# Attention 1 of a two-layer kernel: q and k turned once per feature block in the projection, stacks of the heads filled by SBUF transfers, another order of the pieces, values in halves

## The chip, the cores and the metric

One core of a Trainium2 chip (trn2) runs the whole program. The metric is the device time of one execution in microseconds. The kernel before takes 2137.48 us, the median of 3 runs (2134.89 to 2144.37). Five engines work side by side and meet at semaphores: TensorE (PE; its weight loads are PEld), VectorE (DVE), ScalarE (ACT), GpSimd (POOL) and SyncE (SP), whose queue issues the transfers, one after the other.

## The reference

Two transformer layers on a hidden state of 1 x 1024 x 512 float32: a decayed linear attention, a gated feed-forward with LoRA, a causal softmax attention with ALiBi and a normalisation of q and k, and a feed-forward with GELU. The change is in the third of these, which is

```python
qkv = clip(hidden @ w_qkv.T, -8, 8)             # 512 features each, 32 heads of 16
q = layer_norm(q, q_ln_w, q_ln_b)               # over all 512 features, then split into heads
k = layer_norm(k, k_ln_w, k_ln_b)
scores = q @ k.T / sqrt(16) + alibi_bias        # per head, 1024 x 1024, causal
out = softmax(scores) @ v                       # then @ w_out.T
```

## The kernel before

`stage_attention1` (L822) has three blocks with their own semaphores and a barrier between them: `attention1_qkv` (L836), `attention1_heads` (L1074) and `attention1_out` (L1443).

**Projection, `attention1_qkv`.** 24 tiles m (8 token tiles each for q, k, v) of 128 tokens by 512 features. PE makes a tile with 12 matmuls into PSUM bank m % 8. DVE clips it into `cl` (L944) and takes the moments (L947, L949); POOL makes 1/std and shift in three tiny operations (`moments`, L890 to L894); ACT normalises (L923); POOL multiplies by the weight (`scale`, L899), DVE adds the bias (`shift`, L935) and so writes `q1` and `k1`, tokens on partitions. v is clipped straight into `v1` (L951). POOL also splits each of the three weight matrices into a high and a low part (`split`, L876): that of v comes at m == 3 of the loop over moments.

**Heads, `attention1_heads`.** The 32 heads go in 16 pairs p and 8 quads g (pairs 2g and 2g + 1). For a pair there is a stack `KTs[p % 5]` and a stack `QT[p % 5]`: 128 rows by 1024 tokens, 64 rows for each head: 16 rows of slopes, positions and the row maximum (row `MAXROW`), and three times 16 rows of high and low parts of k or q. A stack is made in three steps: POOL's `gather` (L1126) puts the columns of the pair, split, beside the constants in `ks`, `qs`, tokens on partitions, two pairs per quad; PE's `turn` (L1310) transposes them in 16 transposes (L1318) into a score slot `S[at % 2]`; ACT's `turned` (L1176) copies each to its stack (L1182). A score slot is two PSUM banks, and there are two of them, shared with the scores.

For each pair the row maxima come first. PE makes 24 `piece`s (L1345, matmul at L1354) of 128 queries by up to 512 keys into one of three banks `M[at % 3]`; DVE takes each one's maximum (L1239 with the causal mask on the diagonal, L1243 without). After the last piece DVE combines them (L1247), PE transposes the result (`max_row`, L1363), DVE copies it to `crow` (L1256), and SP writes it by two transfers (L1121) into row MAXROW of `QT`. Only then may the scores of that pair start: `score` (L1322) waits for `max_in` at n == 0.

A quad has 12 steps n (key tile by query range, `STEPS`) times 2 pairs = 24 units u. Unit u: PE makes the scores of two heads (L1334), ACT takes exp into `pr[n % 4]` (L1193), POOL zeroes the triangle of a diagonal step (`select`, L1158), and PE multiplies by `v1` (`values`, L1385: 8 passes for 4 heads side by side in the array, into bank `O`). Between the units PE issues the pieces of the pairs 2g + 2 and 2g + 3, from the generator `maxima(g)`, as many per unit as `paced(g)` says. ACT copies `O` out twice a quad (L1201), PE transposes it (L1371), DVE divides (L1265, L1268). Before the first quad come the turns of pairs 0, 1, 2 and the pieces of pairs 0 and 1: the prologue. Every engine takes its instructions strictly in the order written.

Of the kernel before, what the change touches and what calls it, by code (L numbers as in the profile page):

```python
# [821 lines left out]
def stage_attention1(nc, top, a):  # L822

    ctx = ExitStack()
    with ctx:
        def sb(name, shape, dt=F32):
            return ctx.enter_context(nc.sbuf_tensor(f"a1_{name}", shape, dt))
        q1, k1 = sb("q1", [P, NT, D]), sb("k1", [P, NT, D])
        v1 = sb("v1", [P, NT, H1, DH1 + 1])
        attention1_qkv(nc, top, q1, k1, v1, a["a1_wqkv"], a["a1_ln"])  # L830
        attn = sb("attn", [P, NT, D])
        attention1_heads(nc, top, q1, k1, v1, attn, a)
        attention1_out(nc, top, attn, a["a1_wout"])


def attention1_qkv(nc, top, q1, k1, v1, w_dram, ln_dram):  # L836
# [3 lines left out]
    with ctx:  # L840
# [7 lines left out]
        wb = sb("wb", [P, 4, D])  # L848
        R = 4
        FIRST = 3  # L850
        cl = sb("cl", [P, R, D])
        st, mv = sb("st", [P, R, 6]), sb("mv", [P, R, 2])
# [5 lines left out]
        def whole(m):  # L858

            return (q1, k1)[m // NT][:, m % NT, :]  # L860
# [4 lines left out]
        def _(sp):  # L865
            for c in range(3):
# [3 lines left out]
                if c == 0:  # L870
                    for i in range(4):
                        sp.dma_start(wb[:, i, :], ln_dram[i:i + 1, :].to_broadcast([P, D])).then_inc(s("wb_in"), 16)

        @block.gpsimd
        def _(pool):
# [21 lines left out]
            def scale(m):  # L897
                pool.wait_ge(s("normed"), m + 1)
                nc.gpsimd.tensor_tensor(cl[:, m % R, :], cl[:, m % R, :], wb[:, 2 * (m // NT), :], ALU.mult  # L899
                                        ).then_inc(s("scaled"), 1)  # L900
# [6 lines left out]
            pool.wait_ge(s("wb_in"), 64)  # L907
            for m in range(QK + 1):
                if m < QK:
                    moments(m)  # L910
                if m >= 1:
                    scale(m - 1)
                if m == 3:
                    pool.wait_ge(s("proj_done"), NT)
                    split(2)

        @block.scalar
        def _(act):
            ln_scalar(nc, act, s, b)
            for m in range(QK):  # L920
                r = m % R
                act.wait_ge(s("sh"), m + 1)
                nc.scalar.activation(cl[:, r, :], cl[:, r, :], ACT.Identity, bias=sh[:, r:r + 1],  # L923
                                     scale=rs[:, r:r + 1]).then_inc(s("normed"), 1)

        @block.vector
        def _(dve):
# [3 lines left out]
            dve.wait_ge(s("wb_in"), 64)  # L931

            def shift(m):
                dve.wait_ge(s("scaled"), m + 1)
# [858 lines left out]
```

## Time and profile before

| | us |
|---|---|
| median of 3 runs (lowest, highest) | 2137.48 (2134.89, 2144.37) |
| the profiled execution, its time | 2137.82 |
| its span, first to last instruction | 2136.1 |
| projection of attention 1, from its weights' DMA to its last DVE instruction | 1425.1 to 1517.8 |
| prologue of the heads, from SP's first DMA to the first score | 1519.0 to 1560.3 |
| quad 0 to quad 7, from the first score to the last output | 1560.3 to 1893.8 |
| PE, DVE, ACT, POOL busy over the span | 93%, 41%, 21%, 39% |

The page has a line for each engine with its busy time, the span in 40 slices with the clock that TensorE was granted (full is 2.4 GHz; the records know this level and 1.2 GHz), the waits, and the groups of instructions by line. A line of a timeline gives the start, the busy time and, in brackets, how long the engine was idle before it and who released it. "issue to landing" is the time from the start of a DMA instruction on SP to the last byte's semaphore.

### The profile page before, as it was taken

What the parts mean: (1) busy time and instruction counts of PE and PEld (TensorE: products, weight loads), DVE (VectorE), ACT (ScalarE), POOL (GpSimd) and SP (SyncE); (2) the same over time, 40 slices, a digit from 0 to 9 for tenths busy, and PEclk for the clock granted to TensorE, in tenths of its full rate; (3) what the DMA queues carried; (4) which work ended last, traced back from release to release, by engine and by line L of the source; (5) the groups of instructions that cost most, each with busy time, mean ns of one, the idle gap of its engine ahead of it and who ended that gap; (6) DMA issues with size and microseconds to landing.
All of it is one profiled execution on the core that took longest, in us unless ns stands there. A gap on an engine that the chain in (4) does not pass through costs nothing. (4 is left out here: it accounts for less than half of the span.)

```text
span 2136.1 us, 27055 instructions
## 1 busy us (share of the span) xinstructions
PE 1987.8 (93%) x10154; PEld 1538.6 (72%) x10154; DVE 875.7 (41%) x1593; ACT 453.2 (21%) x550; POOL 831.7 (39%) x1164
## 2 busy tenths in 40 slices
PE   6999999999999999999996799979699889887998
PEld 5888888888888888888885577757444444355877
DVE  4242442323424334243245433335565666524232
ACT  3111111111111111111110200012135555532111
POOL 4331321322313122223000688868513232127765
PEclk9999999999999999999999899989769888897999
DMA  4110110101001101011001233321100000002333
GB/s 149 38 45 28 55 55 27 54 27 54 30 24 54 54 27 54 27 54 34 7 12 40 73 106 96 110 71 40 18 1 1 1 2 1 2 20 77 91 93 99
DMA packets 47564, 98.90 MB, mean 46 GB/s; under 512 B 12976, under 2 KB 17712, under 8 KB 43024
## 3 DMA queue, kind: packets, MB, share of 16 engines
q1 hardware_dynamic: 47504, 98.12, 14.4%
q8 instruction: 36, 0.59, 0.1%
q14 instruction: 24, 0.20, 0.0%
HBM read 95.87 MB, written 2.10 MB: 46 GB/s over the span
## 5 line engine op out<-in xcount | busy, mean ns | idle before, releaser
L60 POOL TENSOR_TENSOR tick<-neg_half 128x1 f32<-128x1 f32 x188 | 53.4, 284 | 669.5 <-PE a_ps L148 615.5
L146 PE MATMUL a_ps<-a_xh_h,a_w_h 128*128 128x512 f32 x768 | 307.4, 400 | 4.6 <-POOL a_w_l L270 3.2
L148 PE MATMUL a_ps<-a_xh_h,a_w_l 128*128 128x512 f32 x768 | 301.6, 393 | 0.0
L147 PE MATMUL a_ps<-a_xh_l,a_w_h 128*128 128x512 f32 x768 | 300.7, 392 | 0.0
L390 DVE TENSOR_TENSOR x<-x,a_ps 128x1024 f32<-128x1024 f32 x64 | 78.2, 1221 | 259.9 <-PE a_ps L148 259.9
L1193 ACT ACTIVATE a1h_pr<-a1h_ps 128x1024 f32<-128x1024 f32 (+1 forms) x192 | 150.0, 811 | 154.7 <-PE a1h_ps L1334 128.5
L146 PEld LDWEIGHTS a_ps<-a_xh_h,a_w_h 128*128 128x128 f32 x768 | 145.0, 189 | 32.8 <-issue 3.5
L148 PEld LDWEIGHTS a_ps<-a_xh_h,a_w_l 128*128 128x128 f32 x768 | 144.5, 188 | 30.4
L147 PEld LDWEIGHTS a_ps<-a_xh_l,a_w_h 128*128 128x128 f32 x768 | 144.9, 189 | 28.0
L1158 POOL TENSOR_SCALAR_AFFINE_SELECT a1h_pr<-a1h_pr 128x256 f32<-128x256 f32 x128 | 51.6, 407 | 261.4 <-ACT a1h_pr L1193 260.6
L1354 PE MATMUL a1h_ps<-a1h_KT,a1h_QT 64*128 64x512 f32 (+2 forms) x384 | 127.8, 472 | 17.6 <-DVE a1h_mx L1243 5.9
L1239 DVE CUSTOM_DVE_ANT_0 a1h_masked<-a1h_ps,a1h_mask 128x128 f32<-128x128 f32 (+3 forms) x256 | 112.9, 485 | 71.0 <-PE a1h_ps L1354 70.5
L372 DVE SCALAR_TENSOR_TENSOR a_gt<-a_th,a_ps 128x1024 f32<-128x1024 f32 x32 | 39.1, 1221 | 234.3 <-ACT a_sq L307 234.3
L251 POOL TENSOR_TENSOR a_w_l<-a_raw,a_w_h 128x2048 fp32r<-128x2048 f32 x29 | 133.7, 4609 | 2.4
L146 PE MATMUL f_ps<-f_xh_h,f_w_h 128*128 128x512 f32 x304 | 121.6, 400 | 7.6 <-DVE f_low_st L728 3.1
L147 PE MATMUL f_ps<-f_xh_l,f_w_h 128*128 128x512 f32 x304 | 121.1, 398 | 0.0
L148 PE MATMUL f_ps<-f_xh_h,f_w_l 128*128 128x512 f32 x304 | 120.8, 397 | 0.0
L316 ACT ACTIVATE a_qT<-a_ps 128x1024 f32<-128x1024 f32 x32 | 32.8, 1024 | 397.4 <-PE a_ps L148 397.4
L1354 PEld LDWEIGHTS a1h_ps<-a1h_KT,a1h_QT 64*128 64x128 f32 x384 | 66.2, 222 | 61.0 <-DVE a1h_mx L1239 24.7
L1334 PEld LDWEIGHTS a1h_ps<-a1h_QT,a1h_KT 64*128 64x128 f32 x384 | 44.5, 217 | 91.0 <-issue 38.4
L146 PE MATMUL a_ps<-a_o_h,a_g_h 128*128 128x512 f32 x256 | 102.9, 402 | 6.2 <-DVE a_g_l L381 5.6
L1243 DVE TENSOR_REDUCE a1h_mx<-a1h_ps 128x1 f32<-128x512 f32 x128 | 84.4, 687 | 55.8 <-PE a1h_ps L1354 55.8
(191 smaller groups left out, 4147.8 us busy)
## 6 DMA issues: line engine op xcount, KB each, us to landing
a_raw<-in_a_wqkgv SPq DMA_DIRECT2D x30, 1024.0 KB, 5.1
f_raw<-in_f_w SPq DMA_DIRECT2D x66, 320.0 KB, 3.1
f_raw<-in_f_w SPq DMA_DIRECT2D x64, 256.0 KB, 2.6
a_raw<-in_a_wout SPq DMA_DIRECT2D x32, 256.0 KB, 5.1
a_cst<-in_a_cst SPq DMA_DIRECT2D x32, 129.0 KB, 2.1
a1q_raw<-in_a_wqkv SPq DMA_DIRECT2D x3, 1024.0 KB, 4.9
x<-in_x_in SPq DMA_DIRECT2D x8, 256.0 KB, 3.8
a_v_nat<-in_a_wqkgv SPq DMA_DIRECT2D x2, 1024.0 KB, 10.6
```

Source lines behind the costliest of these rows:

```text
L60: nc.gpsimd.tensor_tensor(top["tick"][:, :], top["neg_half"][:, 0:1], top["neg_half"][:, 1:2], ALU.mult)
L146: nc.tensor.matmul(out, w_hi, x_hi, start=start, stop=False)
L147: nc.tensor.matmul(out, w_hi, x_lo, start=False, stop=False)
L148: return nc.tensor.matmul(out, w_lo, x_hi, start=False, stop=stop)
L251: nc.gpsimd.tensor_tensor(w_l[:, j, :], raw[:, 0:W4], w_h[:, j, :], ALU.subtract).then_inc(s("w_ready"), 1)
L390: nc.vector.tensor_tensor(a, a, UNIT[(i + 1) % 2], ALU.add).then_inc(s("out_added"), 1)
L1158: nc.gpsimd.affine_select(tri, tri, [[0, 2], [1, P]], ALU.is_ge, 0.0, base=0, channel_multiplier=-1).then_inc(s("selected"), 1)
L1193: nc.scalar.activation(pr[n % SLOTS][:, 2 * i:2 * i + 2, 0:width], S[at % 2][:, :, skip:skip + width], ACT.Exp, scale=0.25).then_inc(s("sc ...
L1239: nc.vector.tensor_tensor_reduce(out=masked[:, at % 3, 0:width], in0=M[at % 3][:, 0:width], in1=mask[:, BANK - width:], scale=-1.0, scalar ...
L1243: nc.vector.tensor_reduce(to, M[at % 3][:, 0:width], AX.X, ALU.max, negate=True).then_inc(s("max_taken"), 1)
L1334: last = nc.tensor.matmul(out[:, h, 0:w], KTs[p % SETS][rows, kt * P:(kt + 1) * P], QT[p % SETS][rows, q0 + width - w:q0 + width], start=True,
L1354: nc.tensor.matmul(out[:, 0:w], QT[p % SETS][rows, t * P:(t + 1) * P], KTs[p % SETS][rows, c * BANK:c * BANK + w], start=True, stop=True). ...
```

## The change

**Projection.** `scale` and `shift` go. ACT's normalised tiles stay in `cl` (8 slots instead of 4). For four token tiles and one block of 128 features PE makes a `turn` of four transposes into one of two banks (PROJ + u % 2); 16 such units, placed after tiles m = 7, 8, 10, 11, 14, 15, 18, 19, two after each. ACT applies weight and bias, now one number per partition, and writes the high part (`high`); DVE makes the full value (`whole`); POOL subtracts (`low`). Result: `q_h`, `q_l`, `k_h`, `k_l`, features on partitions. The projection uses 6 banks instead of 8. v's `split` comes at m == 8.

**Heads.** `gather`, the 16 transposes per pair and the two ACT copies go. SP's `stack(p)` fills the stacks by transfers from SBUF to SBUF of 16 rows by 4 KB: 12 per pair, and 4 of 2 or 3 rows for the slopes; for the first five pairs also 4 of 16 rows with the constants, with two waits for them. `max_row(p)` of SP keeps its two transfers; both stand on the same queue. Pieces alternate wide and narrow; the prologue holds the first 8 pieces of pair 2 (AHEAD), and each quad works 8 pieces ahead. `values` of wide steps is made in two halves at units u - 3. `masked` is bf16.

```diff
 def attention1_qkv(...)
-        R = 4
+        R = 8
         FIRST = 3
+        PROJ = 6
+            def low(u):
+                pool.wait_ge(s("full"), u + 1)
+                nc.gpsimd.tensor_tensor(target(u, "_l"), full[:, u % 2, :], target(u, "_h"), ALU.subtract
+                                        ).then_inc(s("turned_lo"), 1)
-            for m in range(QK + 1):
-                if m < QK:
-                    moments(m)
-                if m >= 1:
-                    scale(m - 1)
-                if m == 3:
+            for m in range(QK):
+                moments(m)
+                for u in units(m):
+                    low(u)
+                if m == 8:
                     pool.wait_ge(s("proj_done"), NT)
                     split(2)
+            def whole(u):
...
+                if u >= 2:
+                    dve.wait_ge(s("turned_lo"), u - 1)
+                nc.vector.tensor_scalar(full[:, u % 2, :], ps[:, PROJ + u % 2, :], wb[:, 2 * c, feature:feature + 1],
+            def turn(u):
+                _, first, feature = TURNS[u]
+                pe.wait_ge(s("normed"), first + 4)
+                if u >= 2:
+                    pe.wait_ge(s("full"), u - 1)
...
+                if m >= PROJ:
+                    pe.wait_ge(s("clipped"), m - PROJ + 1)
                 for k in range(KT):
                     part(m, k)
+                for u in units(m):
+                    turn(u)
```

```diff
 def attention1_heads(...)
+            def stack(p):
+
+                if p >= PAIRS:
+                    return
+                if p >= SETS:
+                    g, i = divmod(p - SETS, 2)
+                    sp.wait_ge(s("score_made"), score_at(g, NS - 1, i) + 1)
+                    sp.wait_ge(s("max_made"), MAX_AT[(p - SETS, NP - 1)] + 1)
+                landed = s(f"stack_in{p % SETS}")
+                for h in range(2):
...
+                    for n, (k, q) in enumerate((("k_h", "q_h"), ("k_l", "q_h"), ("k_h", "q_l"))):
+                        sp.dma_start(kT[at[n]:at[n + 1], :], turned[k].bitcast(F32)[rows, block, :]).then_inc(landed, 16)
+                        sp.dma_start(qT[at[n]:at[n + 1], :], turned[q].bitcast(F32)[rows, block, :]).then_inc(landed, 16)
+                    if p == 0 and h == 0:
+                        sp.wait_ge(s("slopes_round"), 2)
+                    e, r = 2 * p + h, ROWS * h
+                    if p < SETS:
+                        sp.dma_start(kT[r:r + AUG, :], qslope.bitcast(F32)[KBASE:KBASE + AUG, :]).then_inc(s("base_in"), 16)
+                        sp.dma_start(qT[r:r + AUG, :], qslope.bitcast(F32)[QBASE:QBASE + AUG, :]).then_inc(s("base_in"), 16)
+                        sp.wait_ge(s("base_in"), 32 * e + 32)
+                    sp.dma_start(kT[r + 3:r + 5, :], kslope.bitcast(F32)[2 * e:2 * e + 2, :]).then_inc(landed, 16)
+                    sp.dma_start(qT[r:r + 3, :], qslope.bitcast(F32)[3 * e:3 * e + 3, :]).then_inc(landed, 16)
...
+            sp.dma_start(raw[0][:, :], a["a1_qslope"]).then_inc(s("slope_in"), 16)
+            sp.dma_start(raw[1][0:2 * H1, :], a["a1_kslope"]).then_inc(s("slope_in"), 16)
+            stack(0)
+            sp.dma_start(mask[:, :], a["a1_mask"]).then_inc(s("mask_in"), 16)
+            sp.dma_start(later[:, :], a["a1_later"]).then_inc(s("later_in"), 16)
+            for p in range(1, SETS):
+                stack(p)
+            max_row(0)
+            max_row(1)
+            for g in range(QUADS - 1):
+                max_row(2 * g + 2)
+                stack(2 * g + 5)
+                max_row(2 * g + 3)
+                stack(2 * g + 6)
...
 PE, within a quad: for u, upto in enumerate(paced(g))
                     score(g, n, i)
-                    if u == 0:
-                        turn(2 * g + 3)
-                    for _ in range(upto - made):
+                    for _ in range((upto - made + 1) // 2):
+                        next(strand)
+                    before = (u - 3) // 2
+                    if before >= 0:
+                        values(g, before, (u - 3) % 2)
+                    elif g:
+                        values(g - 1, NS + before, (u - 3) % 2)
+                    for _ in range((upto - made) // 2):
                         next(strand)
                     made = upto
-                    if i == 0 and n >= 2:
-                        values(g, n - 2)
...
-                    if u == 15:
-                        turn(2 * g + 4)
...
             def maxima(g):
+                yield from pieces(p, AHEAD, 16)
                 if g:
                     yield output(g - 1, 1)
+                yield from pieces(p, 16, NP)
                 yield from pieces(q, 0, 2)
                 if p < PAIRS:
                     yield max_row(p)
+                yield from pieces(q, 2, 8)
                 yield output(g, 0)
+                yield from pieces(q, 8, NP)
+                yield from pieces(q + 1, 0, 2)
+                if q < PAIRS:
+                    yield max_row(q)
+                yield from pieces(q + 1, 2, AHEAD)
```

## Rows read from the trace of the kernel before

**Rows 1.** The page: span, busy times, and granted clock in tenths by slice of the span.

```profile
span 2136.1 us, 27055 instructions
...
PE 1987.8 (93%) x10154; PEld 1538.6 (72%) x10154; DVE 875.7 (41%) x1593; ACT 453.2 (21%) x550; POOL 831.7 (39%) x1164
...
PEclk9999999999999999999999899989769888897999
```

**Rows 2.** Busy time by stretch: stretch, length, engines with counts, granted clock, DMA.

```profile
1518.90:1560.30 41.40, 29.61 (x97) 18.85 (x98) 22.66 (x81) 7.96 (x9) 13.68 (x40) 0.62 0.18 23
1560.30:1617.10 56.80, 54.67 (x283) 26.15 (x282) 30.79 (x108) 26.34 (x32) 13.70 (x37) 0.73 0.00 1
1617.10:1658.60 41.50, 37.20 (x234) 17.72 (x234) 26.29 (x89) 23.33 (x30) 13.30 (x36) 0.88 0.01 2
...
1826.30:1866.10 39.80, 33.63 (x194) 13.76 (x194) 23.22 (x74) 19.41 (x26) 6.46 (x16) 0.79 0.00 1
1866.10:1893.80 27.70, 22.49 (x162) 7.79 (x162) 1.74 (x6) 18.61 (x26) 6.01 (x15) 0.88 0.00 1
```

**Rows 3.** Who waited for whom, 1617 to 1866: total us, times, longest.

```profile
ACT a1h_pr L1193 <- PE a1h_ps L1334: 110.6, 78, 4.1
DVE a1h_mx L1243 <- PE a1h_ps L1354: 44.2, 48, 2.7
DVE a1h_masked L1239 <- PE a1h_ps L1354: 38.1, 28, 3.9
```

**Rows 4.** Groups by line, 1617 to 1866: count, busy, mean ns, idle before.

```profile
L1318 PE MATMUL a1h_ps<-ident,a1h_ks 128*128 128x128 f32 x80 | 11.0, 281 | 1.1 <-ACT a1h_pr L1193 1.1
L1318 PE MATMUL a1h_ps<-ident,a1h_qs 128*128 128x128 f32 x80 | 10.8, 278 | 0.0
L1182 ACT CAST a1h_KT<-a1h_ps 128x1024 fp32r<-128x1024 f32 x10 | 10.1, 1012 | 2.8 <-PE a1h_ps L1318 2.8
```

**Rows 5.** Timeline of PE and DVE: the projection, its end, the first turn.

```profile
1453.66 0.60 PE L139 MATMUL a1q_ps<-ident,a1q_xn 128*128 128x128 f32 x4
1454.02 0.48 PE L146 MATMUL a1q_ps<-a1q_w_h,a1q_xh_h 128*128 128x512 f32 x1
...
1509.37 0.39 PE L148 MATMUL a1q_ps<-a1q_w_h,a1q_xh_l 128*128 128x512 f32 x1
...
1514.08 3.67 DVE L951 TENSOR_SCALAR a_v<-a1q_ps 128x512 f32<-128x512 f32 x6
...
1527.23 1.94 PE L1318 MATMUL a1h_ps<-ident,a1h_ks 128*128 128x128 f32 x8 [17.48 <-POOL a1h_qs L1152]
...
1532.61 0.50 PE L1354 MATMUL a1h_ps<-a1h_KT,a1h_QT 64*128 64x256 f32 x3
```

**Rows 6.** Groups by line and shape in the projection, 1425 to 1518.

```profile
L899 POOL TENSOR_TENSOR a1q_cl<-a1q_cl,a1q_wb 128x512 f32<-128x512 f32 x16 | 20.5, 1286 | 0.0
...
L944 DVE TENSOR_SCALAR a1q_cl<-a1q_ps 128x512 f32<-128x512 f32 x16 | 10.9, 679 | 0.0
...
L54 POOL TENSOR_SCALAR a1q_w_h<-a1q_raw 128x512 fp32r<-128x512 f32 x12 | 7.5, 621 | 2.1 <-DMA a1q_raw<-in_a_wqkv 2.1
```

**Rows 7.** Timeline of SP: start, time of the group of issues, line, count.

```profile
1.72 3.28 SPq L201 DMA_DIRECT2D x<-in_x_in  x7
...
1863.66 1.31 SPq L1121 DMA_DIRECT2D a1h_QT<-a1h_crow  x2
```

**Rows 8.** DMA issues of the whole span: count, KB each, us to landing.

```profile
a1h_mask<-in_a_mask SPq DMA_DIRECT2D x1, 256.0 KB, 3.9
...
a1h_later<-in_a_later SPq DMA_DIRECT2D x1, 64.0 KB, 2.5
```

**Rows 9.** Timeline of PE: a score behind its row of maxima, and values of two widths.

```profile
1712.66 0.63 PE L1385 MATMUL a1h_ps<-a1h_pr,a_v 128*17 128x256 f32 x8
...
1734.37 1.05 PE L1385 MATMUL a1h_ps<-a1h_pr,a_v 128*17 128x512 f32 x8
...
1866.13 0.68 PE L1334 MATMUL a1h_ps<-a1h_QT,a1h_KT 64*128 64x512 f32 x4 [2.27 <-DMA a1h_QT<-a1h_crow]
```

More of the change, by code:

```diff
@@ L856, in attention1_qkv, with units, target @@
         QK = 2 * NT
-        def whole(m):
-            return (q1, k1)[m // NT][:, m % NT, :]
+        def units(m):
+            return [u for u, (at, _, _) in enumerate(TURNS) if at == m]
+        def target(u, part):
+            _, first, feature = TURNS[u]
+            c, t = first // NT, first % NT
+            return turned["qk"[c] + part][:, feature, t * P:t * P + BANK]
         by_head = lambda ap: ap.rearrange("p (h d) -> p h d", h=H1)
@@ L1003, with count @@
 NP = len(PIECES)
+AHEAD = 8
 def counted():
[L1008 to L1016 removed]
+    at = {}
+    def count(*item):
+        at[item] = len(at)
     def pieces(p, k0, k1):
         for k in range(k0, k1 if p < PAIRS else k0):
[L1020 to L1026 removed]
+            count(p, k)
@@ L1027, in counted @@
     pieces(0, 0, NP)
     pieces(1, 0, 2)
-    other("row", 0)
+    count("row", 0)
     pieces(1, 2, NP)
+    pieces(2, 0, 2)
+    count("row", 1)
+    pieces(2, 2, AHEAD)
     for g in range(QUADS):
-        for n in range(NS):
-            score(g, n, 0)
-            if n == 0:
-                turned(2 * g + 3)
-            score(g, n, 1)
-            if n == 7:
-                turned(2 * g + 4)
         p, q = 2 * g + 2, 2 * g + 3
-        pieces(p, 0, 2)
-        other("row", 2 * g + 1)
-        pieces(p, 2, 18)
+        pieces(p, AHEAD, 16)
@@ L1043, in counted @@
         if g:
-            other("out", g - 1, 1)
-        pieces(p, 18, NP)
+            count("out", g - 1, 1)
+        pieces(p, 16, NP)
         pieces(q, 0, 2)
         if p < PAIRS:
-            other("row", p)
-        pieces(q, 2, 10)
-        other("out", g, 0)
-        pieces(q, 10, NP)
-    other("out", QUADS - 1, 1)
-    return score_at, max_at
-SCORE_AT, MAX_AT = counted()
-def paced(g):
-    first = MAX_AT[("row", 2 * g + 1)] - (2 if g < QUADS - 1 else 0)
-    last = MAX_AT[("row", 2 * g + 3)] - 2 if g < QUADS - 2 else MAX_AT[("row", 2 * g + 3)] if g < QUADS - 1 else len(MAX_AT) - 1
-    worth = [PIECES[i[1]][3] + 80 if isinstance(i[0], int) else 300 for i in list(MAX_AT)[first:last]]
-    marks = [sum(worth[:i]) / sum(worth) for i in range(len(worth))]
-    length = 2 * sum(2 * n + 100 for _, _, n in STEPS)
-    upto, now = [], 1500
+            count("row", p)
@@ new lines, in counted @@
+        pieces(q, 2, 8)
+        count("out", g, 0)
+        pieces(q, 8, NP)
+        pieces(q + 1, 0, 2)
+        if q < PAIRS:
+            count("row", q)
+        pieces(q + 1, 2, AHEAD)
+    count("out", QUADS - 1, 1)
+    return at
+MAX_AT = counted()
+def paced(g):
+    if g == QUADS - 1:
+        return [0] * 3 + [1] * 9 + [2] * 12
+    items = list(MAX_AT)
+    first = MAX_AT[(2 * g + 2, AHEAD)]
+    last = MAX_AT[(2 * g + 4, AHEAD)] if g < QUADS - 2 else MAX_AT[("row", 2 * g + 3)] + 1
+    worth = [PIECES[i[1]][3] + 70 if isinstance(i[0], int) else 350 for i in items[first:last]]
+    length = sum(2 * n + 100 for _, _, n in STEPS) * 2
+    upto, now = [], 0
@@ L1069, in paced, with attention1_heads @@
             now += 2 * n + 100
-            upto.append(sum(m * length < now for m in marks))
-    return upto[:-1] + [len(marks)]
-def attention1_heads(nc, top, q1, k1, v1, attn, a):
+            upto.append(sum(sum(worth[:i]) * length < now * sum(worth) for i in range(len(worth))))
+    return upto
+def attention1_heads(nc, top, turned, v1, attn, a):
     ctx = ExitStack()
@@ L1205, in _ @@
             nc.scalar.copy(laterb[:, :], later[:, :]).then_inc(s("later_ready"), 1)
-            for p in range(3):
-                turned(p)
             for g in range(QUADS):
@@ L1417, in _ @@
             max_row(0)
-            turn(2)
             for k in range(2, NP):
                 piece(1, k)
+            piece(2, 0)
+            piece(2, 1)
+            max_row(1)
+            for k in range(2, AHEAD):
+                piece(2, k)
             for g in range(QUADS):
```

294 lines of the change are left out of this document (124 added, 170 removed).

## Prediction

> **What bounds the kernel now.** I read the page first [rows 1]. PE is busy 93% of the span, the others 41% and less, so PE's order of work sets the end. The clock line gives 9 nearly everywhere and falls to 7 and 6 in slices 29 and 30 and in some slices behind them: that is the attention the change is about. The table by stretch splits it [rows 2]: a prologue of 41.4 us, quad 0 of 56.8 us, quads like the one shown of 41.5 us (1617.1 to 1826.3 is five of them, 209.2 us), quad 6 of 39.8 and quad 7 of 27.7 us. In a quad of 41.5 us PE is busy 37.2, DVE 26.3, ACT 23.3 us. PE's busy time there counts the latency of matmuls that come singly, so it is no proof of a full array; the waits say what happens [rows 3]: ACT waits for scores 110.6 us and DVE for pieces 44.2 + 38.1 = 82.3 us of 249. Both starve behind PE's one ordered stream, in which turns, scores, values and pieces take turns. PE's order bounds the quads; in the prologue DVE's maxima do (22.7 us busy of 41.4, nearly all after the first turn), and before them a hole of 17.5 us in PE between the last projection matmul and the first turn [rows 5].
>
> **Projection.** PE's last matmul ends at 1509.8, DVE's last clip at 1517.75, 8 us behind [rows 5]. The change adds 16 units of four transposes to PE. Four transposes keep it 0.36 us from the next matmul (1453.66 to 1454.02) and 0.60 us if it must let them finish [rows 5]: 5.8 to 9.6 us; I take 5.8, since matmuls follow most units. DVE loses 16 adds and gains 16 reads of a bank, each like the clip of 0.68 us [rows 6], and this comes out even. POOL loses 16 multiplications of 1.29 us and gains 16 subtractions of the same shape and price [rows 6]. But they come in twos, and the split of v, four times 0.62 + 1.29 = 7.6 us [rows 6], now stands at m = 8 with the moments of tiles 9 to 11 queued behind it on POOL. DVE's `whole` waits for `low` and holds the clips behind it; PE's turn at m = 14 waits for normalised tile 11. I put 3 us of PE's waits there, between 0 and 6. PE then ends at 1509.8 + 5.8 + 3 = 1518.6, and DVE's last clip (0.68) right behind it, at 1519: against 1517.75 it is +1 us, between -2 and +4. The smaller weight and bias transfers lie beside the layer norm: nothing either way.
>
> **Prologue: what SP must issue before the first score.** This is the heart. Before, the first score starts at 1560.3. After, SP's queue reads: two loads, stack(0), two loads, stacks 1 to 4, and only then max_row(0) and max_row(1). The first score waits for the row of pair 0. Durations: an issue takes 3.28/7 = 0.47 us for 128 rows of 2 KB, and 1.31/2 = 0.66 us for the one kind that goes from SBUF to SBUF [rows 7]. The trace has no transfer of 16 rows by 4 KB. Its bounds are 0.34 (an estimate: under the nearer row by as much as 128 rows cost more than 16, if a quarter of the 0.47 goes with the rows) and 0.66; I take 0.46, because it is as plain in its pattern as those of 0.47, and 0.66 for the two slope transfers of a head. A wait for landing: 64 KB from DRAM land 2.5 us after their issue began [rows 8]; the row of maxima lets its score start at 1866.13, 2.47 us after its pair of transfers began at 1863.66 [rows 7, 9]. I take 2.0 us for 64 KB inside SBUF, so 1.5 us beyond the issue itself. A head in the first five pairs: 8 x 0.46 + 1.5 + 2 x 0.66 = 6.5 us; a stack 13.0 us. Stack(0) starts with six issues and waits until POOL has rounded the slopes: loads issued at 1519.0 and 1519.5 of 512 and 256 KB land in about 4 us (256 KB: 3.9 [rows 8]), two operations of twice 0.62 us [rows 6], so 1526.5; then 2 x 0.46 + 1.5 + 2 x 0.66 = 3.7 us to finish that head, 6.5 us for the other: 1536.7; two loads, 0.9: 1537.6; four stacks, 52: 1589.6; the row of pair 0, 2.5: **the first score at about 1592, 32 us later than now.** DVE doesn't reach this: 56 pieces instead of 48 at (1560.3 - 1532.6)/48 = 0.58 us [rows 2, 5], from 1540 when the mask is in, would be over at 1573. With 0.34 us an issue, 16 x 0.12 less five times, it is 1582; with 0.66 us, 16 x 0.2 more five times, 1608. The gather, six turns and six copies of the prologue cost nothing any more, but the hole they made is replaced by this longer one.
>
> **A quad, without waits for SP.** PE loses the turns: (11.0 + 10.8)/5 = 4.4 us of 37.2 busy. ACT loses four copies of 1.01 us, 4.05 us [rows 4], and with them two waits of the score slots. Values in halves add work: two halves of 256 take 2 x 0.63 against 1.05 us for 512 [rows 9], 0.2 us at most for each of eight wide steps, 0 to 1.7 us; the lower end is likely, since the halves stand between pieces. In return PE comes back to the scores and pieces sooner. Floors: DVE 26.3 us; ACT 23.3 - 4.05 = 19.3 us. Ceiling: 41.5 - 4.4 = 37.1 us, where no wait goes. I take 33 us, PE's remaining busy time 32.8 us with idle and saved latency even; between 28.5 (DVE nearly full) and 37.1. `masked` in bf16 and POOL without gather: nothing, because DVE's operation reads PSUM at the same width and POOL's gather stood beside the quads, not in their way.
>
> **The new wait in each quad.** On SP, stack(2g + 5) waits for the last score of pair 2g, the unit before the last of quad g, then issues 16 transfers: 12 x 0.46 + 4 x 0.66 = 8.2 us. The row of pair 2g + 3 is queued behind it, and its 2.5 us come on top: 10.7 us after that score. Yet score(g + 1, 0, 1), the second unit of the next quad, waits for this row. Until there PE has one score, the next quad's first score, three halves of values and some six pieces, which DVE takes at 0.58 us: 3.5 us. PE stalls some 7 us, and DVE, ACT and the rest of the values are queued behind it. A stall of this length has a price in clock: after the hole of 17.5 us the stretch is granted 0.62, and quad 0 0.73, against 0.88 later [rows 2, 5]. I add 2 us (0 to 4). This happens behind quads 0 to 5; for g = 6 there is no stack to issue. With issues of 0.34 to 0.66 us, the stall is 5 to 10.
>
> **The sum.** Prologue +32. Quad 0: 33 + 9 + 3 for the low clock at its start = 45 against 56.8: -11.8. Quads 1 to 5: 42 against 41.84: +0.8. Quad 6: 34 against 39.8: -5.8. Quad 7, without pieces and mostly ACT's: 26 against 27.7: -1.7. Projection +1. Together +14.5 us. The execution profiled took 2137.82 us (the median is 2137.48; I leave out the 0.3): **2152 us**.
>
> **The rivals.**
> *A, DVE becomes the bound (the other side: faster).* If finer interleaving fills DVE, a quad goes at 28.5 us. For it: DVE idles 82 us in six quads only because PE serves it in lumps [rows 3]. Against it: PE in order, clock at 0.88. Seven quads save 4.5 us each: 2152 - 31.5 = 2120.5. The whole is faster than now if a quad without waits goes under 31.0 us, and counts as faster by over 0.5% under 29.4.
> *B, a transfer of 16 rows is dearer than a plain one.* For it: the only SBUF to SBUF rows cost 0.66 us [rows 7]. Then a stack of the prologue takes 3.2 us more, five times, and each stall 2.4 us more, six times: +30, 2182 us. The Trainium skill has a mechanism that would do the same: by its page SBUF — State Buffer, Door 1: The DMA port swizzle, a transfer's rate goes with how many of 16 ports its partitions reach, and 16 neighbouring partitions reach 4, some 109 GB/s. An estimate by that page is 0.60 us for 64 KB, longer than the issue that I took, and the sum would be near 2173; no row here shows a transfer of so few long rows.
> *C, quads don't shrink beyond PE's own saving.* Each takes 37.1 us, as ACT's waits for scores stay [rows 3]: +4.1 us seven times, 2181 us.
>
> **How the numbers follow.** Forecast 0.45, with 2136 to 2168 of its own; A 0.25; B 0.15; C 0.15. About 0.5% (10.7 us) is what a measurement of this kernel can tell from no change. Faster by more: A, less a little: 0.24. Within: the lower part of the forecast's range, up to 2148, and A's edge: 0.21. Slower by more: the rest of the forecast, B, C: 0.55. The range has to reach both sides: from 2112, A with most of its width, to 2190, B and C with theirs; less than 2 in 10 stays outside.
>
> **What would show it.** SP's timeline: 16 issues between the last score of pair 2g and the transfers of `crow`; right if a stack takes 7 to 9 us, wrong under 5.5. PE's waits: score L1334 of the second unit, released by the DMA of `crow`, some 7 us six times, and none behind quad 6; if these are missing, the main term is wrong. The first score at 1582 to 1608. Between the stalls, a quad of 33 us by the table of stretches; at 29 A has it, at 37 C. Timeline of the projection: PE's waits at m = 14 for `a1q_cl`. Clock by stretch: under 0.8 behind each stall. The prediction fails if transfers land so that the row is never last, or if DVE, not SP, still releases the first score.

## The result and the profile after the change

The changed kernel takes **2193.66 us** (median of 4 runs, 2192.41 to 2196.30), the kernel before 2137.81 us in the same comparison (4 runs): the ratio is 1.0259 [1.0233, 1.0284]. The forecast was 2152 us in a range of 2112 to 2190: the sign is right, the time forecast is 42 us short, and the time lies just past the range.

The page of the changed kernel, with two groups of its section on the costliest:

```profile
span 2190.9 us, 27811 instructions
...
PE 1952.5 (89%) x10474; PEld 1519.5 (69%) x10474; DVE 878.3 (40%) x1593; ACT 438.4 (20%) x534; POOL 773.7 (35%) x1006
...
PEclk9999999999999999999997999989558878887999
...
L1346 PE MATMUL a1h_ps<-a1h_QT,a1h_KT 64*128 64x512 f32 (+2 forms) x384 | 114.8, 457 | 91.7 <-DMA a1h_QT<-a1h_crow 91.3
...
L1366 PE MATMUL a1h_ps<-a1h_KT,a1h_QT 64*128 64x512 f32 (+2 forms) x384 | 143.4, 482 | 42.8 <-DMA a1h_QT<-a1h_qslope 32.1
```

PE is busy 35 us less than in [rows 1], and the span is 54.8 us longer: PE has less to do and waits. Scores (L1346) wait 91.3 us for `crow`, pieces (L1366) 32.1 us for a stack. The clock row shows two slices at 5, where before the lowest was 6.

The table by stretch, with the columns of [rows 2]: prologue, quad 0, two of the quads 1 to 5, quad 6, and quad 7 (its last 3 us lie behind the quad). As in [rows 2], every boundary behind the prologue is the score of a quad's second unit, so each stall lies at the end of the stretch before it:

```profile
1527.10:1618.60 91.50, 26.09 (x58) 14.36 (x58) 28.55 (x99) 1.88 (x3) 2.05 (x2) 0.52 0.41 72
1618.60:1673.70 55.10, 44.66 (x291) 19.56 (x291) 28.52 (x90) 20.96 (x26) 6.95 (x17) 0.72 0.10 17
1673.70:1717.00 43.30, 32.26 (x266) 14.75 (x266) 26.19 (x88) 20.20 (x26) 6.53 (x16) 0.82 0.24 40
...
1846.70:1890.00 43.30, 32.28 (x265) 14.62 (x266) 25.98 (x86) 20.21 (x26) 6.53 (x16) 0.82 0.24 40
1890.00:1921.80 31.80, 29.74 (x258) 12.96 (x258) 21.85 (x74) 19.58 (x26) 6.12 (x15) 0.88 0.01 2
1921.80:1950.00 28.20, 24.88 (x229) 9.66 (x230) 2.05 (x6) 19.21 (x27) 6.53 (x16) 0.86 0.01 1
```

Set beside [rows 2], the whole difference can be laid out. Each entry is the stretch after less the stretch before. Quad 7 ends at ScalarE's last copy of an output, which starts at 1892.06 us before and at 1946.78 us after. The changed kernel's projection began 2.1 us sooner in this execution (its first transposition at 1426.41 us, before at 1428.54, and between 1427.3 and 1430.3 in the runs below), so the stage itself grew by 10.3 us.

| stretch | forecast | measured | how |
|---|---|---|---|
| projection | +1 | +8.2 | 1527.1 - 1518.9 |
| prologue | +32 | +50.1 | 91.5 - 41.4 |
| quad 0 | -11.8 | -1.7 | 55.1 - 56.8 |
| quads 1 to 5 | +0.8 | +7.1 | 216.3 - 209.2 |
| quad 6 | -5.8 | -8.0 | 31.8 - 39.8 |
| quad 7 | -1.7 | -1.0 | 25.0 - 26.0 |
| sum | +14.5 | +54.7 | the spans differ by 54.8 |

The timeline of PE shows the two long waits of the prologue, then the second and the sixth of the waits for a row that end a quad; there are six of 10.1 to 10.5 us, and behind quad 6 one of 0.2:

```profile
1550.36 0.98 PE L1366 MATMUL a1h_ps<-a1h_KT,a1h_QT 64*128 64x512 f32 x3 [25.04 <-DMA a1h_QT<-a1h_qslope]
...
1618.67 0.80 PE L1346 MATMUL a1h_ps<-a1h_QT,a1h_KT 64*128 64x512 f32 x2 [29.69 <-DMA a1h_QT<-a1h_crow]
...
1717.05 0.80 PE L1346 MATMUL a1h_ps<-a1h_QT,a1h_KT 64*128 64x512 f32 x2 [10.19 <-DMA a1h_QT<-a1h_crow]
...
1890.00 0.80 PE L1346 MATMUL a1h_ps<-a1h_QT,a1h_KT 64*128 64x512 f32 x2 [10.20 <-DMA a1h_QT<-a1h_crow]
```

The timeline of SP shows what stands ahead of them: in the prologue (first load, first constant rows after POOL has rounded the slopes, the mask behind stack 0, the rows of pairs 0 and 1), and in a quad (first and last issue of a stack, then the row):

```profile
1527.12 0.33 SPq L1177 DMA_DIRECT2D a_attn<-in_a_qslope  x1
...
1536.24 0.51 SPq L1164 DMA_DIRECT2D a1h_KT<-a1h_qslope  x1
...
1548.87 0.41 SPq L1180 DMA_DIRECT2D a1h_mask<-in_a_mask  x1
...
1616.18 2.68 SPq L1174 DMA_DIRECT2D a1h_QT<-a1h_crow  x4
...
1704.24 0.55 SPq L1158 DMA_DIRECT2D a1h_KT<-a_k_h  x1
...
1713.81 0.69 SPq L1168 DMA_DIRECT2D a1h_QT<-a1h_qslope  x1
1714.54 1.34 SPq L1174 DMA_DIRECT2D a1h_QT<-a1h_crow  x2
```

A transfer of 16 rows is issued every 0.60 to 0.63 us. A stack of a quad takes 1714.54 - 1704.24 = 10.3 us, and the score starts 2.5 us behind the issue of its row. Of the 91.5 us of the prologue, 21.8 pass up to the mask, 66.4 with the four other stacks (from 1549.8), and 2.5 with the row.

### The profile page after: what moved, and what is told of

Same layout as the page of the kernel before. It is cut to its first block and busy times, and to the rows that moved or that the text cites. A ratio compares the mean times of both kernels' runs of the same rounds, so it can differ in the third digit from the quotient of the medians.

```text
span 2190.9 us, 27811 instructions
## 1 busy us (share of the span) xinstructions
PE 1952.5 (89%) x10474; PEld 1519.5 (69%) x10474; DVE 878.3 (40%) x1593; ACT 438.4 (20%) x534; POOL 773.7 (35%) x1006
## 5 line engine op out<-in xcount | busy, mean ns | idle before, releaser
L1346 PE MATMUL a1h_ps<-a1h_QT,a1h_KT 64*128 64x512 f32 (+2 forms) x384 | 114.8, 457 | 91.7 <-DMA a1h_QT<-a1h_crow 91.3
L1366 PE MATMUL a1h_ps<-a1h_KT,a1h_QT 64*128 64x512 f32 (+2 forms) x384 | 143.4, 482 | 42.8 <-DMA a1h_QT<-a1h_qslope 32.1
L148 PEld LDWEIGHTS a_ps<-a_xh_h,a_w_l 128*128 128x128 f32 x768 | 144.4, 188 | 30.3
L1261 DVE CUSTOM_DVE_ANT_0 a1h_masked<-a1h_ps,a1h_mask 128x384 bf16<-128x384 f32 (+3 forms) x256 | 115.3, 486 | 99.2 <-PE a1h_ps L1366 98.1
L1366 PEld LDWEIGHTS a1h_ps<-a1h_KT,a1h_QT 64*128 64x128 f32 x384 | 72.7, 220 | 118.3 <-issue 49.9
L1346 PEld LDWEIGHTS a1h_ps<-a1h_QT,a1h_KT 64*128 64x128 f32 x384 | 55.3, 212 | 114.9 <-DMA a1h_QT<-a1h_crow 93.4
```

Of the source, the lines that this page charges most:

```text
L148: return nc.tensor.matmul(out, w_lo, x_hi, start=False, stop=stop)
L1261: nc.vector.tensor_tensor_reduce(out=masked[:, at % 3, 0:width], in0=M[at % 3][:, 0:width], in1=mask[:, BANK - width:], scale=-1.0, scalar ...
L1346: last = nc.tensor.matmul(out[:, h, 0:w], KTs[p % SETS][rows, kt * P:(kt + 1) * P], QT[p % SETS][rows, q0 + width - w:q0 + width], start=True,
L1366: nc.tensor.matmul(out[:, 0:w], QT[p % SETS][rows, t * P:(t + 1) * P], KTs[p % SETS][rows, c * BANK:c * BANK + w], start=True, stop=True). ...
```

## The experiments

**What an issue costs.** The kernel before, with unused transfers in series on SP in one quad; between series SP waits until all have landed.

```diff
+                for i in range(8):
+                    sp.dma_start(probe[16 * i:16 * i + 16, 1, :], probe[0:16, 0, :]).then_inc(s("probe_in"), 16)
+                sp.wait_ge(s("probe_in"), 16 * 8)
+                for i in range(8):
+                    sp.dma_start(probe[16 * i:16 * i + 16, 1, :], d[0][0:16, 0:1024]).then_inc(s("probe_in"), 16)
...
```

> The kernel before with transfers added that nothing uses, on SP in quad 1, where its queue is idle: 8 of 16 rows by 4 KB from SBUF to SBUF, 8 of 16 rows by 4 KB from DRAM, 4 of 128 rows by 4 KB from SBUF, 4 of 128 rows by 4 KB from DRAM, 4 of 64 rows from SBUF, 8 of 16 rows by 256 bytes from SBUF, 4 of 2 rows by 4 KB from SBUF; SP waits for each series to land. Nothing of the kernel's own work waits for them, as long as the whole series takes under 35 us. Theory S (the source decides the issue): both series from DRAM take 0.45 us an issue, all from SBUF 0.63. Theory N (the number of rows decides): 128 rows take 0.45, from either side, and 16 rows 0.63, from either side. Theory D (the data hold the issue up): 256-byte rows are issued in under 0.5 us, 4 KB rows in 0.63.

The timeline of SP; a row is a series, its second number the time from its first issue to the end of its last. The shapes are 16 rows of 4 KB out of SBUF, the same out of DRAM, 128 rows of 4 KB out of SBUF and out of DRAM, 64 rows of 4 KB, 16 rows of 256 B and 2 rows of 4 KB, the last three out of SBUF:

```profile
1613.38 5.94 SPq L1122 DMA_DIRECT2D a1h_probe<-a1h_probe  x8
1621.05 3.59 SPq L1125 DMA_DIRECT2D a1h_probe<-in_a_wqkv  x8
1626.42 3.27 SPq L1128 DMA_DIRECT2D a1h_probe<-a1h_probe  x4
1633.26 1.90 SPq L1131 DMA_DIRECT2D a1h_probe<-in_a_wqkv  x4
1641.83 3.17 SPq L1134 DMA_DIRECT2D a1h_probe<-a1h_probe  x4
1648.53 4.98 SPq L1137 DMA_DIRECT2D a1h_probe<-a1h_probe  x8
1654.61 2.47 SPq L1140 DMA_DIRECT2D a1h_probe<-a1h_probe  x4
```

Divided by the count: 0.74, 0.45, 0.82, 0.48, 0.79, 0.62 and 0.62 us. Out of DRAM the pitch is 0.45 to 0.48, whether 64 or 512 KB. Out of SBUF it is 0.62 even for 4 KB, and more where much is moved. So it is the source that sets the least price of an issue, not the number or length of the rows: theory S. It is one execution, and why its series of 64 KB goes at 0.74 us where the stacks' transfers of the same size go at 0.60 to 0.63 was not tried. The forecast's 0.46 was the price of the wrong source; the floor of rival B (0.66, the one kind from SBUF) was the right neighbour.

**The row ahead of the stack.** One pair of lines in SP's loop changes places; nothing else.

```diff
-                stack(2 * g + 5)
                 max_row(2 * g + 3)
+                stack(2 * g + 5)
                 stack(2 * g + 6)
```

> The kernel after, with one line moved on SP: in the loop over quads max_row(2g + 3) stands ahead of stack(2g + 5) instead of behind it. Theory Q (the queue: the second score of a quad waits because 16 transfers of 0.63 us stand ahead of its row of maxima): PE's six waits of 10.2 us at the second unit go down to under 1 us each, a quad goes from 43.3 to about 33 us, and the time from 2193.7 to about 2132 us, 61 us less. Rival R (the quads are long for another reason, and the wait only collects what PE would lose to DVE, ACT or late stacks): the wait moves to another line, the quads stay over 40 us and the time over 2175 us. The prologue stays as it is: first score near 1619 us.

2123.03 us, ratio to before 0.9926 [0.9898, 0.9954]: 70.6 us under the changed kernel. The six waits are gone; what is left of PE's waits for `crow` is the one at the first score. The waits, and two quads in the table by stretch:

```profile
PE a1h_ps L1346 <- DMA a1h_QT<-a1h_crow: 30.5, 2, 29.6
...
1686.90:1717.20 30.30, 28.96 (x260) 13.23 (x258) 25.57 (x88) 19.87 (x26) 6.50 (x16) 1.00 0.33 57
1717.20:1748.00 30.80, 29.48 (x269) 13.41 (x266) 26.11 (x88) 20.28 (x26) 6.50 (x16) 1.00 0.33 56
```

The waits removed were 91.3 - 30.5 = 60.8 us. The other 10 us go with the clock: a quad of 43.3 us less its wait of 10.2 is 33.1 us at a granted clock of 0.82, and here it is 30.3 to 30.8 us at 1.00; five such quads are 12 to 14 us. The chain from SP's queue over the row to the score is shown, and its price with it.

**The rows of the prologue earlier.** The rows of pairs 0 and 1 go behind stack 2 instead of behind stack 4.

```diff
-            for p in range(1, SETS):
-                stack(p)
+            stack(1)
+            stack(2)
             max_row(0)
             max_row(1)
+            stack(3)
+            stack(4)
```

> The kernel after, with the order of SP in the prologue changed: stack(1), stack(2), max_row(0), max_row(1), stack(3), stack(4), instead of the four stacks first. Theory Q: the first score is then released after stack 2 has landed (near 1584), two pieces, row 1 and its landing: at about 1590 instead of 1618.7, and the time falls by about 28 us, to 2165 us. Rival R (stacks 3 and 4 are needed early as well, or DVE's 56 pieces are what takes this long): the first score stays within 5 us of 1618, or the gain is lost again in quad 0; time over 2185 us. The six waits of 10 us between the quads stay in both.

2166.61 us, ratio 1.0127 [1.0098, 1.0155]: 27 us less than the changed kernel. The prologue, from SP's first load to the first score, takes 60.9 us (1530.77 to 1591.63) instead of 91.6 (1527.12 to 1618.67), 30.7 us less. In the prologue SP's queue is what the kernel waits for, and 27 of these 30.7 us come back in the time.

**Both orders.** 

> Both changes of SP's order, in one kernel. Theory Q: the two gains add, 61 + 28 us: about 2105 us, under the kernel before (2137.8) by 1.5%. Rival R: they don't add, because stacks 3 and 4 now land in quad 0 and hold its pieces: 2120 us or more.

2090.53 us, ratio 0.9768 [0.9740, 0.9796]: with two changes of order the changed kernel beats the kernel before by 2.3%. It is also 15 us below its own forecast of 2105, as the first order alone was 9 us below its 2132: both forecasts had counted the waits and left out what the quads behind them gain in clock. Its quad 0 and two quads behind it:

```profile
1591.60:1634.90 43.30, 42.99 (x271) 18.90 (x271) 27.57 (x89) 19.54 (x25) 6.11 (x15) 0.71 0.31 53
1634.90:1666.00 31.10, 29.76 (x268) 13.38 (x268) 25.81 (x86) 20.29 (x27) 6.42 (x16) 1.00 0.32 54
1666.00:1696.90 30.90, 29.54 (x271) 13.43 (x272) 26.09 (x88) 20.20 (x27) 6.52 (x17) 1.00 0.33 56
```

Quad 0 has no wait for a row here and is still 12.4 us longer than a quad behind it: PE is busy 43.0 against 29.5 us with as many matmuls (271), at 0.71. That goes with starting the quad on the lower of the two levels (1.2 GHz), on which PE had been through the prologue (busy 25.5 of 60.9 us, granted clock 0.50).

**Values whole, pieces by tile.** Two edits of the change taken back, each alone, on top of both orders.

```diff
-                whole = kt == 0 or width == P
+                whole = True
```

> The two edits of SP's order, and the products with the values of every step done whole, as before the change, instead of in halves between the scores. It prices the halves. A quad of the run with the order alone takes 30.7 us with TensorE busy 29.5, so whoever thinks the quad TensorE-bound expects no more than a microsecond in all: 2090 us (2088 to 2094). Rival (the halves give VectorE's maxima time between the scores and so made a part of the fall from 41.6 to 30.7 us): 1 us more for each of eight quads, 2099 us (2095 to 2105).

> The two edits of SP's order, and the pieces of maxima in the order of before, tile by tile. It prices the reordering. Theory (a quad without the wait is TensorE-bound at 29.5 of 30.7 us, and three banks of maxima smooth out single wide pieces): within 4 us, 2092 us (2088 to 2096). Rival (wide pieces in a row let VectorE, 0.4 to 0.7 us each, hold TensorE up at the banks): 2 us more in each of seven quads, 2105 us (2098 to 2112), with TensorE's waits for max_taken over 10 us in all.

For the second, `PIECES` is the list of before. Both are set against the kernel with both orders (2090.53 us, 0.9768 [0.9740, 0.9796]), of which they differ by that one edit. Values whole: 2110.39 us, ratio 0.9860 [0.9825, 0.9895], 20 us more. The rival had the direction, but less than half the size. Pieces by tile: 2099.19 us, ratio 0.9800 [0.9766, 0.9834]: 7 to 9 us more, but the intervals overlap, so that no price of the reordering is shown; the time lies between the two expectations. Values whole, by stretch:

```profile
1635.10:1667.80 32.70, 29.47 (x215) 13.05 (x215) 26.65 (x89) 20.31 (x27) 7.02 (x18) 1.00 0.32 53
...
1700.70:1734.70 34.00, 31.36 (x204) 13.45 (x202) 26.27 (x89) 19.92 (x26) 6.41 (x16) 0.90 0.30 50
```

Pieces by tile:

```profile
1667.20:1698.40 31.20, 29.35 (x268) 13.07 (x266) 26.34 (x88) 20.32 (x26) 6.41 (x17) 1.00 0.32 55
...
1764.00:1801.30 37.30, 35.95 (x268) 15.57 (x267) 26.26 (x88) 20.18 (x27) 6.37 (x16) 0.77 0.26 45
```

At full clock the halves are worth some 1.7 us a quad (32.7 against 30.9 to 31.1) and the order of the pieces 0.3 us (31.2 against 30.9). The rest of what was lost goes with the clock: with values whole PE was idle 3.2 us of the first quad shown instead of 1.3, and of the four behind it one was granted 0.95 and three 0.90, the one shown 1.3 us longer; with pieces by tile one late quad was granted 0.77 and took 37.3 us. The kernel with both orders has one such quad too, the fifth (0.95). That the additional idle time is what drew the clock down was not tested by itself.

**The split of v, tile by tile, in the projection.**

```diff
-                if m == 8:
+                if 8 <= m < 12:
                     pool.wait_ge(s("proj_done"), NT)
-                    split(2)
+                    split(2, (m - 8,))
```

In the changed kernel the chain is read from the timelines of four engines, from its end back to its start:

```profile
1486.47 0.87 PE L1002 MATMUL a1q_ps<-ident,a1q_cl 128*128 128x128 f32 x3 [6.52 <-DVE a1q_full L963]
...
1485.51 1.53 DVE L963 TENSOR_SCALAR a1q_full<-a1q_ps,a1q_wb 128x512 f32<-128x512 f32 x2 [7.51 <-ACT a_q_h L939]
...
1484.00 0.81 ACT L949 ACTIVATE a1q_cl<-a1q_cl,a1q_sh,a1q_rs 128x512 f32<-128x512 f32 x1 [10.79 <-POOL a1q_sh L905]
1484.72 1.43 ACT L939 ACTIVATE a_q_h<-a1q_ps,a1q_wb 128x512 fp32r<-128x512 f32 x2
...
1474.85 0.63 POOL L54 TENSOR_SCALAR a1q_w_h<-a1q_raw 128x512 fp32r<-128x512 f32 x1
...
1481.42 1.26 POOL L894 TENSOR_TENSOR a1q_w_l<-a1q_raw,a1q_w_h 128x512 fp32r<-128x512 f32 x1
1482.77 0.19 POOL L901 TENSOR_SCALAR a1q_ve<-a1q_mv 128x1 f32<-128x1 f32 x1
```

PE's turn (L1002, at m = 11) waits for `full` on DVE, that for `high` on ACT (L939), which is queued behind a normalisation (L949), which waits for POOL's moments (L901), which stand behind 7.8 us of splitting. The edit is made on top of both orders.

> Two edits of SP's order as in the run of 2090.5 us, and in the projection the split of v's weights on GpSimd taken apart: one tile of it (hi and lo) behind the moments of each of m = 8, 9, 10, 11, where all four stood behind those of m = 8. Theory P (the projection's growth of 7 us over the forecast is GpSimd's split of v standing ahead of the moments of m = 9, behind which ScalarE's turned copies queue and with them TensorE's turns): TensorE's wait of 8.0 us for a1q_full at the turn of m = 11 shrinks below 3 us, the heads' part starts about 5 us sooner, 2085 us (2082 to 2088). Rival (the wait is the length of the chain ScalarE high, VectorE full, GpSimd low per turn, whatever the split does): the same time is waited in smaller pieces, 2090 us (2088 to 2093).

PE's wait there falls from 8.0 us (in the kernel with both orders) to 2.2, its waits for `full` in all from 10.3 to 6.0. The first piece starts at 1548.92 instead of 1553.88, 4.96 us sooner; 0.7 us of this is a projection that began sooner, so that 4.3 us are left. The median does not show it: 2091.42 us, ratio 0.9778 [0.9739, 0.9818]. The spans of the profiled executions fell by 4.0 us (2093.2 to 2089.2). So the step is shown in the trace; its worth in time is not, and three pairs of profiled executions, below, are what there is.

**One landing wait for the constant rows of a stack.** On top of both orders; the first five stacks send the data of both heads first.

```diff
-                        sp.wait_ge(s("base_in"), 32 * e + 32)
...
+                    sp.wait_ge(s(f"base_in{p}"), 64)
```

The line that goes stood in the loop over the two heads; the new one comes once, behind both heads' data.

> The two edits of SP's order, and inside a stack of the first five the data of both heads go first, then the constant rows of both with one wait for their landing instead of one for each head, then the slopes. Nothing else is changed. Theory S (the prologue is SP's series of issues and waits): in the first stack the second head's six transfers (3.8 us) lie beside the rounding of the slopes, and a landing wait of some 2 us goes from every stack: the first piece starts 4 to 6 us sooner and the first score 8 to 10 us sooner, 2082 us (2079 to 2085). Rival (the prologue past its first piece is bound by VectorE's and TensorE's pieces at half clock, busy 24 to 26 of the 36 us there): only the first piece moves, 2086 us (2085 to 2089).

2082.92 us, ratio 0.9726 [0.9694, 0.9758]. The first piece starts at 1546.47 and the first score at 1580.43, 11.2 us sooner than with both orders (1591.65); 2.5 us of this is a projection that began sooner (1427.29 against 1429.80), so the edit gave 8.7 us, and the ratio says 9. SP still set the prologue.

**Two queues.** On top of the one landing wait, ScalarE issues stacks 1 and 3 (first run), the same with the split of v apart (second), or the Q side of each of the first five stacks, with the split apart (third). Of the first run's edit, SP's lines and ScalarE's:

```diff
-            for p in range(1, SETS):
-                stack(p)
+            stack(sp, 2)
             max_row(0)
             max_row(1)
+            stack(sp, 4)
...
+            stack(act, 1)
...
+            stack(act, 3)
```

> The kernel of 2082.9 us (rows of maxima ahead of stacks, one landing wait for the constant rows of a stack), with stacks 1 and 3 of the first five issued from ScalarE's queue instead of SP's. Theory S (after the first stack the prologue still waits for SP's series: 1.8 and 1.2 us ahead of the first pieces of stacks 1 and 2): both waits go, the first score comes 3 us sooner, 2080 us (2078 to 2082). Rival (transfers of two queues share the 16 DMA engines, busy 0.4 of the time there, and each lands later): the first piece moves to 1 us or more later than in that kernel and nothing is gained, 2083 us (2082 to 2087).

> The kernel with two queues, and the split of v's weights taken apart by tile as in an earlier run, where the first piece came 4.95 us sooner and the median did not show it. Theory P: another 5 us on top of the two queues, 2075 us (2073 to 2078), and TensorE's wait for a1q_full at m = 11 is 2.2 us. Rival (what the projection gives is lost again at the clock of the stages behind it, as the median of that earlier run, 2091.4, against the profiled gain of 4 us may say): 2079 us (2078 to 2082).

> As the run before, but each of the first five stacks is shared: its K side is issued by SP, its Q side by ScalarE, so that six transfers of 0.63 us stand in a queue ahead of the rounding of the slopes instead of twelve. Theory S: the first piece is then bound by the rounding of the slopes (9 us after the first load), two base transfers, their landing and two slopes, 2 us sooner than with the stack in one queue, and the first score some 4 us sooner than in the kernel of 2082.9 us beside the 5 us of the split: 2073 us (2071 to 2077). Rival (ScalarE's issue of an SBUF transfer costs more than SP's 0.59 us, so that its side comes last): the first piece is no sooner, 2077 us or more.

2088.23 us (0.9759 [0.9731, 0.9787]), 2082.12 us (0.9727 [0.9697, 0.9758]) and 2084.73 us (0.9736 [0.9705, 0.9767]), where the forecasts were 2080, 2075 and 2073: none of the three is a gain over the 0.9726 [0.9694, 0.9758] of one queue, and their intervals overlap with it. The rival holds. In the first of them the first piece waits 27.26 us, where one queue had 19.63. Its timelines of ACT and SP, and the table by stretch:

```profile
1531.60 0.60 ACTq L1157 DMA_DIRECT2D a1h_QT<-a_q_h  x1
...
1537.66 1.35 ACTq L1157 DMA_DIRECT2D a1h_QT<-a_q_h  x1
...
1544.16 1.23 SPq L1162 DMA_DIRECT2D a1h_KT<-a1h_qslope  x1
```

```profile
1533.20:1544.20 11.00, 0.00 (x0) 0.00 (x0) 0.00 (x0) 0.00 (x0) 2.05 (x2) 0.55 1.05 161
1557.00:1567.00 10.00, 7.02 (x19) 4.25 (x16) 7.59 (x25) 0.30 (x1) 0.00 (x0) 0.50 0.98 148
```

The first issues of each queue go at 0.6 us, then most of both take 1.1 to 1.35, one 1.48: the 16 DMA engines are as good as full (shares of 0.98 to 1.05, 148 to 161 GB/s). With one queue (the kernel of 2082.92 us) a stretch with a stack and pieces has a share of 0.64; its first stack, beside the two loads of the slopes, has 0.94, and every issue of the stack there still takes 0.59 or 0.60 us:

```profile
1530.00:1537.00 7.00, 0.00 (x0) 0.00 (x0) 0.00 (x0) 0.00 (x0) 1.13 (x2) 0.50 0.94 194
...
1563.00:1570.00 7.00, 5.60 (x14) 3.36 (x13) 5.96 (x20) 0.00 (x0) 0.00 (x0) 0.50 0.64 105
```

Stack 0, which everything waits for, now shares them with stack 1. The Trainium skill says it on the page DMA: Bandwidth & Descriptors, section Issuing engines are not separate DMA queues: transfers of several issuing engines end up on the same 16 engines, and a second issuer saves no more than issue time. The trace agrees, with these shares; that the full engines are what stretches the issues was not tested by itself. The Trainium skill's page SBUF — State Buffer, Door 1: The DMA port swizzle, which the forecast weighed, gives 0.60 us for 64 KB as an estimate, near the 0.63 of one queue; but 16 rows of 256 B have a pitch of 0.62 too, so it is not the data that sets that pitch.

The third run lost its time in another way. From the first transposition of the projection to the first score it took 147.0 us, 1.5 less than the kernel on one queue that comes next. But ScalarE issued its side of stacks 3 and 4 ahead of the first exponentials, the last of it at 1583.25, and TensorE stood behind it. The timelines of ACT and PE:

```profile
1583.25 1.45 ACTq L1167 DMA_DIRECT2D a1h_QT<-a1h_qslope  x2
...
1587.10 0.69 PE L1359 MATMUL a1h_ps<-a1h_QT,a1h_KT 64*128 64x384 f32 x2 [8.09 <-ACT a1h_pr L1229]
```

So what is shown is that these three ways to use ScalarE's queue gain nothing. A kernel in which ScalarE issues for the first three stacks only was not tried.

**All that helped, on one queue.** Both orders, the one landing wait, and the split of v apart.

> Rows of maxima ahead of stacks, one landing wait for the constant rows of a stack, the split of v's weights taken apart by tile, and all stacks on SP's queue: the kernel of 2082.9 us with the edit of the projection added. Theory P (the turn at m = 11 waits for GpSimd's split): the first piece comes 5 us sooner than in that kernel for the same start of the projection, the ratio to the kernel before falls from 0.9726 to 0.970 (0.969 to 0.972), 2077 us where the kernel before takes 2140. Rival (what the projection gives is lost at the clock of the stages behind it): the ratio stays at 0.9726 or above.

**2079.56 us**, ratio 0.9702 [0.9671, 0.9733]: 3.0% under the kernel before. The three pairs with and without the split of v differ by 4.0, 4.2 and 3.2 us of profiled span (2093.2 and 2089.2; 2086.1 and 2081.9; 2077.8 and 2074.6): some 4 us each time, though each is a single execution, and executions of one of these kernels lie up to 10 us apart. Against the stacks shared by two queues (the third run above), the first piece starts 1.9 us sooner (1541.88 against 1543.76) and the first score 1.3 us later (1575.78 against 1574.45): nothing that the medians part.

## Why the prediction was right and wrong

**The mechanism was right.** The stacks stand in SP's queue ahead of the rows; the first score and the second unit of each quad up to the sixth wait for them, and none behind quad 6. One swap of two lines gives back 70.6 us, the swap in the prologue 27 us.

**The price of an issue was mis-sized**, and with it three terms. I took 0.46 us "because it is as plain in its pattern as those of 0.47"; the likeness that counted was the source. The row from SBUF (0.66) [rows 7] was the nearer one; it measured 0.63. In the prologue a stack took 16.6 us on average instead of 13.0: 20 issues of 0.60 to 0.75 make 12.8 instead of 10.0 us, two landing waits 3.8 instead of 3.0 us. Four stacks are 66.4 us instead of 52 (+14.4), and the first with its loads and the rounding is 4.1 us longer: together the 18.5 us by which the prologue (91.5) passed the forecast (73, from 1519 to 1592). A stall took 10.2 us instead of 7: the stack 10.3 instead of 8.2, and PE had 2.6 us of work beside it instead of 3.7. Rival B, at 2182 us, was the case that came. Put into the forecast's own sum, 0.63 gives 2178 us: the issue price is 26 of the 42 us, and alone it would have stayed inside the range.

**Quad 0 was mis-sized by 10 us, and the rows had most of it.** I put 3 us for the low clock at its start. The first scores of quads 0 and 1, before and after, the fourth line without the wait that follows it:

```profile
1560.33 1.11 PE L1334 MATMUL a1h_ps<-a1h_QT,a1h_KT 64*128 64x512 f32 x2
...
1610.85 0.50 PE L1334 MATMUL a1h_ps<-a1h_QT,a1h_KT 64*128 64x512 f32 x2
...
1618.67 0.80 PE L1346 MATMUL a1h_ps<-a1h_QT,a1h_KT 64*128 64x512 f32 x2 [29.69 <-DMA a1h_QT<-a1h_crow]
...
1662.22 0.49 PE L1346 MATMUL a1h_ps<-a1h_QT,a1h_KT 64*128 64x512 f32 x2
```

From first score to first score quad 0 took 50.5 us before, 9.0 more than the 41.5 of the next, and 43.6 after, 10.4 more than the 33.1 of a later one with its stall taken off. So the 3 should have been 9 to 10. The 56.8 us of [rows 2], 15.3 over the next quad, say more than this, because that stretch runs on to the second unit of quad 1 and so holds 6.3 us of quad 1; I set 33 + 9 + 3 beside it without this part, which is 1.4 us after. Together: 33.1 + 10.4 + 1.4 and a stall of 10.1 make 55.0 of the 55.1 us. The price of a cold start is to be read off as the first quad less the others, between equal boundaries, not estimated.

**The projection was mis-sized by 7 us, or by 9 from its own start.** The cause named, the split of v on POOL, is right for the longest wait; its place is not. PE did not wait at m = 14 for `a1q_cl`, but at m = 11 for `full` (6.5 us), because ACT serves normalisations and turned copies in one order. Together with 2.3 us for another `full`, 2.1 us for a bank and 0.2 us for a normalised tile, PE waited 11.2 us, where before it waited 3.3 for a bank: 8 more instead of 3. And PE was busy 85.8 instead of 76.4 us there: 9.3 more instead of the 5.8 taken for the turns. PE's end came 17.7 us later from the start of the stage, not 8.8; the stage grew by only 10.3, because DVE's last clip, 8 us behind PE before, now lay right behind it, as forecast.

**A quad without waits** was forecast at 33 us, and 2 more for the clock behind a stall; it came to 33.1 at a granted clock of 0.82 with its stall taken off. In the kernels without the stall it is 30.9, at 1.00. It was better than the 33 taken, not as short as rival A's 28.5: PE, busy 29.5 us of 30.9, bounds it, while DVE has 26.1. Rival C falls. I had the halves add up to 1.7 us a quad and PE's sooner return make up for it; taken back they cost 1.7 us a quad at full clock and 20 us in all. How the remaining fall from 41.5 us parts between the turns, the copies and the gather that went, and the clock (0.88 before), was not tried.

**The range** ended at 2190 because it took rival B with nothing on top. Issue price, projection and the clock of quad 0 are three separate terms, and all three were put too low.

## What to carry to other kernels

When work moves from an engine to transfers, write down the issuing queue as an engine's stream: how many issues, at the price of a row with the same source memory, and who waits for what is queued last. Put the small transfer that someone waits for ahead of the large batch that nobody needs yet: here that is two changes of order, and they turn a kernel 2.6% slower than before into one 2.3% faster. Price an idle TensorE twice, by the wait and by the lower clock of what follows, and read the second from the first stage behind an existing hole, between boundaries that hold the same work. An engine whose queue issues transfers is held by them: before it is given some, look at who waits for its own work behind them (here 8.1 us).

## What the runs showed of the hardware that was not expected

- An issue on SP's queue costs 0.45 to 0.48 us when the source is DRAM, for 64 and for 512 KB, and at least 0.62 us when it is SBUF, even for 4 KB; out of SBUF the pitch grows to 0.74 for a series of 64 KB and 0.82 for 512 KB, in the one execution with such series.
- Two issuing queues that send 64 KB transfers inside SBUF bring the 16 DMA engines to a share of 0.98 to 1.05 at 148 to 161 GB/s, and single issues then take up to 1.48 us. One queue beside two loads from DRAM had a share of 0.94 at 194 GB/s with issues of 0.59 us.
- A quad of 271 matmuls took 30.9 us at a granted clock of 1.00 (2.4 GHz) and 43.3 us at 0.71, behind 60.9 us in which PE had been busy 25.5 us at 0.50 (1.2 GHz).
